# V of two head groups made in the recurrences of a fused four-layer kernel, in place of one

## The reference, cut to what matters

```python
def _cross_attention(q_in, kv_in, wq, bq, wk, bk, wv, bv, wo, bo, bias_k, bias_v):
    qh = (q_in @ wq + bq).reshape(b, q_len, H, K)
    kh = (kv_in @ wk + bk).reshape(b, t, H, K)
    vh = (kv_in @ wv + bv).reshape(b, t, H, K)
    kh = jnp.concatenate([kh, jnp.broadcast_to(bias_k, (b, 1, H, K))], axis=1)
    vh = jnp.concatenate([vh, jnp.broadcast_to(bias_v, (b, 1, H, K))], axis=1)
    logits = jnp.einsum('bqhk,bthk->bhqt', qh, kh) / scale
    weights = jax.nn.softmax(logits, axis=-1)
    ctx = jnp.einsum('bhqt,bthk->bqhk', weights, vh).reshape(b, q_len, H * K)
    return ctx @ wo + bo

x = _L0_xattn_ref(x, ctx_2048, ...)
x = _L1_xattn_ref(x, ctx_2048, ctx_2048, ...)
x = _L2_xattn_ref(ctx_2048, x, mask_BxS2_ik0, ...)
x = _L3_xattn_ref(x, ctx_2048, ...)
```

## Time and profile before

| | |
|---|---|
| median of 3 runs | 3144.73 us (3142.94 to 3148.15) |
| span of the profiled execution | 3143.0 us |
| PE busy (matmuls) | 2966.0 us, 94% |
| PE weight loads busy | 2488.1 us, 79% |
| DVE, ACT, POOL busy | 1326.3, 1117.2, 1030.7 us |
| moved | 289.75 MB, mean 92 GB/s |

### The profile page before, as it was taken

One profiled execution on the slowest core, in us unless ns is written; L12 is line 12 of the kernel. 1 busy time (PEld: TensorE's weight loads), 2 busy tenths in 40 slices (PEclk: granted clock), 3 DMA queues, 4 the chain that ended last, 5 costly groups with the idle time before them and its releaser, 6 DMA issues.

```text
span 3143.0 us, 43370 instructions
## 1 busy us (share of the span) xinstructions
PE 2966.0 (94%) x16412; PEld 2488.1 (79%) x16412; DVE 1326.3 (42%) x3062; ACT 1117.2 (36%) x2541; POOL 1030.7 (33%) x956
## 2 busy tenths in 40 slices
PE   6799888899999999999999999999989999998999
PEld 3445456888998998888989989989878877777887
DVE  4784886433333333433333333333421156563134
ACT  2333345433223222333232222232333355564332
POOL 4674674213113122222121121131245333345420
PEclk8897899999999999999999999999999999999999
DMA  6664651532122122222122222121111111111133
GB/s 214 188 195 164 199 165 44 195 119 106 60 73 106 60 73 87 73 76 78 70 93 74 73 80 73 67 106 60 53 41 67 66 45 45 43 38 58 54 114 94
DMA packets 98260, 289.75 MB, mean 92 GB/s; under 512 B 8552, under 2 KB 55144, under 8 KB 89224
## 3 DMA queue, kind: packets, MB, share of 16 engines
q1 hardware_dynamic: 97576, 286.29, 26.8%
q10 hardware_dynamic: 480, 0.69, 0.1%
HBM read 262.96 MB, written 23.99 MB: 91 GB/s over the span
## 4 chain that ended last, share of the span: by engine, by line
PE 74%; DVE 7%; ACT 6%; POOL 5%; issue 4%; DMA 3%; PEldq 0%; PEld 0%; SPq 0%; ACTq 0%; POOLq 0%; DVEq 0%
PE bank L189 21%; PE bank L191 20%; PE bank L190 20%; PE bank L1908 5%; POOL W_lo L229 3%; PE bank L1893 2%; DMA W_raw<-in_weights 2%; DVE max L2118 1%; ACT W_hi L220 1%; ACT prob L1996 1%; PE bank L2537 1%; DVE prob L2747 1%; PE bank L625 1%; POOL x L1306 1%; ACT prob L2652 1%
## 5 line engine op out<-in xcount | busy, mean ns | idle before, releaser
L2202 POOL TENSOR_SCALAR prob<-prob,inverse 112x376 f32<-112x376 f32 x256 | 144.3, 584 | 1275.1 <-DVE inverse L2124 1275.1
L229 POOL TENSOR_TENSOR W_lo<-W_raw,W_hi 128x1024 fp32r<-128x1024 f32 x138 | 329.1, 2408 | 159.7 <-ACT W_hi L220 156.1
L189 PE MATMUL bank<-ctx_hi,W_hi 128*128 128x376 f32 x1024 | 354.0, 346 | 6.8 <-DVE K_lo L271 4.2
L271 DVE SCALAR_TENSOR_TENSOR K_lo<-bank,vectors,K_hi 128x375 fp32r<-128x375 f32 (+1 forms) x288 | 172.8, 606 | 408.7 <-ACT K_hi L262 408.7
L190 PE MATMUL bank<-ctx_lo,W_hi 128*128 128x376 f32 x1024 | 343.7, 336 | 0.0
L191 PE MATMUL bank<-ctx_hi,W_lo 128*128 128x376 f32 x1024 | 343.2, 335 | 0.0
L189 PE MATMUL bank<-act_hi,W_hi 128*128 128x448 f32 x784 | 300.1, 383 | 10.5 <-DVE act_lo L269 3.6
L2069 DVE TENSOR_TENSOR V<-bank,bv 128x512 f32<-128x512 f32 x168 | 116.3, 692 | 433.6 <-PE bank L1908 235.4
L1996 ACT ACTIVATE prob<-bank,minus 112x376 f32<-112x376 f32 x256 | 143.7, 574 | 434.3 <-DVE minus L2121 434.3
L190 PE MATMUL bank<-act_lo,W_hi 128*128 128x448 f32 x784 | 293.2, 374 | 0.0
L191 PE MATMUL bank<-act_hi,W_lo 128*128 128x448 f32 x784 | 292.7, 373 | 0.0
(11 more groups left out here) (278 smaller groups left out, 6124.1 us busy)
## 6 DMA issues: line engine op xcount, KB each, us to landing
W_raw<-in_weights SPq DMA_DIRECT2D x69, 1024.0 KB, 4.9
ctx_hi<-ctx_split SPq DMA_DIRECT2D x64, 752.0 KB, 4.3
ctx_lo<-ctx_split SPq DMA_DIRECT2D x64, 752.0 KB, 5.8
v_spread<-v_rows SPq DMA_DIRECT2D x88, 224.0 KB
att<-in_ctxT SPq DMA_DIRECT2D x16, 376.0 KB, 5.3
ctx_split<-W_hi SPq DMA_DIRECT2D x16, 376.0 KB, 3.9
ctx_split<-W_lo SPq DMA_DIRECT2D x16, 376.0 KB, 4.9
W_hi<-ctx_split SPq DMA_DIRECT2D x32, 188.0 KB, 4.3
```

Source lines behind the costliest of these rows:

```text
L189: nc.tensor.matmul(dst, left[0], right[0], start=first, stop=False)
L229: pool.tensor_tensor(k.Wl[:, slot, cs, :], k.Wraw[:, cs, :], k.Wh[:, slot, cs, :].bitcast(F32), ALU.subtract).then_inc(*k.w_low.now((n, i)))
L271: dve.scalar_tensor_tensor(out=low, in0=src, scalar=bias, in1=high.bitcast(F32), op0=ALU.add, op1=ALU.subtract).then_inc(*k.banks.draining ...
L2202: pool.tensor_scalar(k.Pm[:, h, :], k.Pm[:, h, :], k.rsum[:, h:h + 1], 1.0, ALU.mult, ALU.mult).then_inc(*k.prob_done.now((n, h)))
```

## The change

`MADE` becomes 2. The fills go batch by batch, both groups of a batch after each other, on the same chunks; two quarter-tiles stand in each filling step, tile by tile. The context slot is cut into five chunks in rotation, so that the first chunk of the next batch is loaded while the present batch's four are read, and each of the others once the last tile of the second group has read the chunk whose place it takes. The second V weight gets a slot of its own (a fifth), is loaded before the first half's steps and split at steps 3 and 5 of it (`VALUES_AT`); the load of the first half's "g" weight moves from before the steps to step 5. Chunk loads are issued in the step of the matmul that frees them and stores one step earlier than they were. The attention units of group 1 become made units. A scratch area for dynamic transfers is made smaller.

```diff
-MADE = 1
-ORDER = (["v", "k", "r", "v1_0", "g", "o", "v", "r", "k"] + [f"v1_{g}" for g in range(1, MADE)] + ["g", "o", "fr", "fk"]
+MADE = 2
+ORDER = (["v", "k", "r"] + [f"v1_{g}" for g in range(MADE)] + ["g", "o", "v", "r", "k", "g", "o", "fr", "fk"]
-NSLOT = 4
+NSLOT = 5
-SLOT = ([0, 1, 0, 2, 1, 0, 1, 1, 0] + [2] * (MADE - 1) + [0, 1, 0, 2]
-        + [3, 1, 0, 2] + [(n + 3) % NSLOT for n in range(len(ORDER) - ORDER.index("q1_1"))])
+SLOT = ([0, 1, 0] + [2, 4] + [1, 0, 1, 1, 0] + [0, 1, 0, 2]
+        + [3, 1, 0, 2] + [3, 0, 2] * (MADE - 1) + [(n + 3) % 4 for n in range(len(ORDER) - ORDER.index(f"q1_{MADE}"))])
...
-FILLS = [(g, b) for g in range(MADE) for b in range(B)]
-QUANTA = [(0, c) for c in range(C)] + [(j, c) for c in range(C) for j in (1, 2)]
+FILLS = [(g, b) for b in range(B) for g in range(MADE)]
+QUANTA = [(j, c) for j in range(3) for c in range(C)]
...
+CHUNKS = 5
+
+def chunk_slot(b, c):
+    return (C * (b % HB) + c) % CHUNKS
...
-        if j == 0:
-            pe.wait_ge(k.chunk_loaded[c], 32 * (f + 1))
+        if j == 0 and g == 0:
+            pe.wait_ge(k.chunk_loaded[chunk_slot(b, c)], 32 * chunk_loads(b, c))
...
-        elif j == 2:
-            m.then_inc(*k.chunk_read.now((f, c)))
+        elif j == 2 and g == MADE - 1:
+            m.then_inc(*k.chunk_read.now((b, c)))
...
-    for q in range(made_until((half, n), 2), made_until((half, n), 1)):
+    for q in range(made_until((half, n), 1), made_until((half, n))):
         f, q = divmod(q, NQ)
-        j, c = QUANTA[q]
-        if j == 2 and (f + 1) % PER_HALF:
-            sp_chunk(k, f + 1, c)
-    for t in range(tiles_of(made_until((half, n), 3)), tiles_of(made_until((half, n), 2))):
+        (j, c), (g, b) = QUANTA[q], FILLS[f]
+        if q == 0 and g == 0 and (b + 1) % HB:
+            sp_chunk(k, b + 1, 0)
+        if j == 2 and g == MADE - 1 and (b + 1) % HB and c < C - 1:
+            sp_chunk(k, b + 1, c + 1)
+    for t in range(tiles_of(made_until((half, n), 2)), tiles_of(made_until((half, n), 1))):
...
+VALUES_AT = (3, 5)
...
+            if half == 0 and n in VALUES_AT:
+                act_split_weight(k, W_VALUES[1], (VALUES_AT.index(n),))
...
+            if half == 0 and n in VALUES_AT:
+                pool_split_weight(k, W_VALUES[1], (VALUES_AT.index(n),))
...
+            sp_load_weight(k, W_VALUES[1])
...
-        sp_load_weight(k, w["g"])
+        if half:
+            sp_load_weight(k, w["g"])
...
+            if half == 0 and n == VALUES_AT[1]:
+                sp_load_weight(k, w["g"])
...
-    nc = _bacc.Bacc("TRN2", target_bir_lowering=False, num_devices=1)
+    nc = _bacc.Bacc("TRN2", target_bir_lowering=False, num_devices=1, dynamic_dma_scratch_size=512)
```

More of the change, by code:

```diff
@@ L217, in act_split_weight, with pool_split_weight @@
         act.wait_ge(*k.banks.filled(("vf", len(FILLS) - 1, 2)))
-    for i in range(2):
+    for i in parts:
         cs = slice(2 * i, 2 * i + 2)
         act.copy(k.Wh[:, slot, cs, :], k.Wraw[:, cs, :]).then_inc(*k.w_high.now((n, i)))
-def pool_split_weight(k, n):
+def pool_split_weight(k, n, parts=range(2)):
     if n >= len(ORDER):
@@ L374, in plan_values, with chunk_loads, context_chunk @@
     for f in fills:
[L375 to L379, removed]
+        k.w_last[W_VALUES[FILLS[f][0]]] = ("vf", f, 2)
+    k.chunk_read.expect([(FILLS[f][1], c) for f in fills if FILLS[f][0] == MADE - 1 for c in range(C - 1)])
+CHUNKS = 5
+def chunk_slot(b, c):
+    return (C * (b % HB) + c) % CHUNKS
+def chunk_loads(b, c):
+    s = chunk_slot(b, c)
+    return sum(chunk_slot(*at) == s for at in CHUNK_ORDER[0:CHUNK_ORDER.index((b, c)) + 1])
+CHUNK_ORDER = [(b, c) for b in range(B) for c in range(C)]
+def context_chunk(k, b, c):
+    cols = slice(SP * chunk_slot(b, c), SP * (chunk_slot(b, c) + 1))
+    return [w[:, CONTEXT_SLOT].rearrange("p c d -> p (c d)")[:, cols] for w in (k.Wh, k.Wl)]
 TILES = [(f, j) for f in range(len(FILLS)) for j in range(3)]
 def tiles_of(quanta):
-    f, q = divmod(quanta, NQ)
-    return 3 * f + (q >= 4) + (q >= 11)
+    return quanta // C
 def pe_fill(k, half, n):
@@ L442, in sp_first_chunk, with chunk_before, sp_chunk @@
             k.nc.sync.wait_ge(k.cx_stored[s], 32 * 4 * (half + 1))
[L443 to L449, removed]
-    sp.dma_start(ch.bitcast(F32), k.cx_dram[b, 0, :, c]).then_inc(k.chunk_loaded[c], 16)
-    sp.dma_start(cl.bitcast(F32), k.cx_dram[b, 1, :, c]).then_inc(k.chunk_loaded[c], 16)
+    sp_chunk(k, HB * half, c)
+def chunk_before(b, c):
+    i = C * (b % HB) + c - CHUNKS
+    return (b // HB * HB + i // C, i % C) if i >= 0 else None
+def sp_chunk(k, b, c):
+    sp, before = k.nc.sync, chunk_before(b, c)
+    if before:
+        b0, c0 = before
+        sp.wait_ge(*(k.chunk_read[before] if c0 < C - 1 else k.banks.filled(("vf", MADE * b0 + MADE - 1, 2))))
+    ch, cl = context_chunk(k, b, c)
+    sp.dma_start(ch.bitcast(F32), k.cx_dram[b, 0, :, c]).then_inc(k.chunk_loaded[chunk_slot(b, c)], 16)
+    sp.dma_start(cl.bitcast(F32), k.cx_dram[b, 1, :, c]).then_inc(k.chunk_loaded[chunk_slot(b, c)], 16)
 def sp_value_store(k, n):
```

12 lines of the change are left out of this document (6 added, 6 removed).

## The result

| | before | after |
|---|---|---|
| median of the runs | 3144.73 us | 3152.36 us (3149.44 to 3156.77, 5 runs) |
| span of the profiled execution | 3143.0 us | 3150.1 us |
| ratio to before on the same chip, 95% interval | | 1.0035 [1.0024, 1.0045] |

The kernel became slower by 0.35%, some 11 us by the ratio. The medians in the table differ by 7.6 us and the two spans by 7.1, where the ratios give 10 to 11; a sum over one pair of traces is good to some 4 us. The forecast was 3146 in a range of 3114 to 3176. The net came out near it, but two of its terms did not, and they erred against each other. That is what the runs had to take apart.

A forecast was written before the change was run, and what follows sets the result against it. It took TensorE alone to bound attention's group 1, and TensorE, VectorE and GpSimd, chained by single-step waits, the recurrences. Terms -52 + 42 + 6 + 5 = +1 us on a 3143.0 span gave 3146 us, range 3114 to 3176.

The forecast's parts named there:

- Attention, -52: Attention stage: group 1's units no longer make V; 40.6 us from six units, 9 and 2.5 from crossings, 52 off.
- The crossing into group 2: Attention stage: this crossing becomes the kind that stood at the crossing into group 1, 34.2 us for 36.7, gaining 2.5.
- the crossing into group 1: Attention stage: this 60.0 us crossing loses 4 tiles of V, 11.0 us; with gaps, a gain of 9 us.
- Early term, 6: First half's steps 1 to 12: second V weight's split and the later load of "g" add 6 us, between 0 and 13.
- The added matmuls, 42: Recurrences, steps 13 to 60: 33.3 us of matmuls per half less 12.5 of some 17 idle used; 42 us on.
- The argument against: Recurrences, against the faster rival: VectorE picks up a block's sums one step after TensorE, so a lag stalls it at once.
- sum for a full clock: Recurrences: with the clock full throughout, TensorE's busy time would shrink by up to 7 + 11 = 18 us.
- The faster rival: Recurrences: TensorE's idle time used almost whole, wait for chunks hidden; halves grow by 25 us, total 3121; chance 0.22.
- The chunks, 5: Recurrences: shorter distance between a chunk's readers costs 0.8 us at each of six batch changes; 5 on, between 0 and 20.
- the slower rival: Recurrences: chunk loads stall TensorE and spreads, 24 us at six changes plus 8 of half clock; 3173; chance 0.22.
- the 0.8 us a turn: Recurrences, each change of batch: low half landing 7.3 us after issue against a distance of some 6.5 us; 0.8 us wait.
- Evictions and stores, 0: Recurrences: 12 more evictions per half on ScalarE and 12 more stored tiles, both hidden, costing nothing unless bursts delay spreads.

The follow-up runs named there:

- one_weight: Changed kernel with both groups using the first V weight, the second's load and split left out and "g" loaded where it was before: 1.0003, 3144.41 us.
- late_weight: Changed kernel with the second V weight loaded at step 10 and split at steps 15 and 16, after "g"; output weight later: 1.0015, 3146.28 us.
- no_reload_third: Changed kernel with no chunk replaced within a half and one matmul in place of three in the second group's quarter-tiles: 0.9871, 3101.77 us.
- no_reload_after: Changed kernel with all fills of a half reading the first batch's chunks, other batches' chunk loads left out: 0.9939, 3125.17 us.
- interleaved: Changed kernel with the second group's tiles 1 and 2 going through the chunks in pairs, freeing two chunks earlier: 1.0004, 3140.84 us.
- stores_later: Changed kernel with SP's stores of finished V tiles issued one step later, as before the change: 1.0000, 3140.22 us.
- all three edits: Changed kernel with the edits of interleaved, stores_later and late_weight together: 0.9977, 3132.18 us; also without chunk loads within a half: 0.9957, 3127.53 us.
- no_reload_before: Kernel before the change, with all fills of a half reading the first batch's chunks, other chunk loads left out: 0.9994, 3141.05 us.

## Why the prediction came out right in its net, and where its steps were wrong

**Attention, -52: right.** It measured -48.3. The six units gave 40.7, to 0.1 us what the comparison of group 0 with group 1 had said, so costing the change by the group that had already been changed was sound, and the matmuls' own 8.3 us a unit would have been too much. The crossing into group 2 gave 2.8 for 2.5. Only the crossing into group 1 was mis-sized, 4.9 for 9: with V gone from it, the weight load and the split that stood beside TensorE's work stand in the chain (7.59 us of load at 809.10), and TensorE is idle 7.7 us in place of 3.7.

**Early term, 6: right.** 6.8, and ScalarE's wait 3.14 for 3.4. one_weight shows that it is the second weight's; in late_weight's trace it goes where the split goes.

**The added matmuls, 42: too large.** Without chunk loads the growth over before is 13.6 + 10.5 = 24 us, and no_reload_third shows that nearly all of it is the 192 matmuls that it leaves out. The term was the added busy time, 66 us, less the idle time used, "12.5 of some 17 us" a half. The idle time was the smaller mistake: TensorE idled 36.5 us in the two stretches before and 7.6 in no_reload_after (121.5 busy of 123.5 us, 117.3 of 122.9), so 29 us were used and not 25. The argument against, that VectorE needs the sums one step later, did not hold at this size. The busy time was the larger one: it grew by 53 us (238.8 less 185.8) and not 66. With the mean granted clock up from 0.92 and 0.88 to 0.95 and 0.97, the prediction's own sum for a full clock (18 us to be had) gives an estimate of 9 of these 13 us; the other 4 are not traced. The prediction held the clock for an argument of the faster rival alone and left it out of its term. That rival, priced at 25 us of growth, had this part right to 1 us, but no sum is given for its 25 (all idle time used gives 31, a full clock 18 less), so the closeness is partly luck. The rule of the Trainium skill that it cited ("Perfetto Trace Analysis", Identifying the Most-Contended Engine), by which weight loads tell the headroom, would have given no growth at all. The trace does not agree: 24 us of growth with weight loads busy 74.5 of 123.5 us. The idle time of the matmul row was the better guide here.

**The chunks, 5: too small, and out of the bounds given (0 to 20).** They cost 27 us, near what the slower rival had said (24 for six turns and 8 of half clock). Its sign was that waits for chunks or spreads exceed 25 us. TensorE's own waits for chunks show 16.2 us and VectorE's for spreads 17 (11.2 in the row above and 6.0 for `tmp`), so neither did. The rest of the 27 us is mostly the clock: in the stretches of after TensorE is idle 22.3 us and busy 251.3, without chunk loads 7.6 and 238.8. So 15 us of the cost are idle time and 12 are the same matmuls taking longer, at 0.94 and 0.92 in place of 0.95 and 0.97 (by the mean clocks, as above, an estimate of 8 of the 12); the matmul at 202.40 is one of those at the half clock. The rival's mechanism was half right. It had the landing as what decides, at about 7 us. The landings measured in after's first half are shorter than before, not longer:

```profile
DMA to landing us min/median/max: 2.5/4.5/7.5
```

4.5 us in the median against 7.3 in the earlier trace rows (5.4 against 7.2 in the second half). The step that failed is the 0.8 us a turn: a landing of 7.3 us less a distance of "2.5 steps, some 6.5 us". At the turn shown above the landing took 5.83 us, and from the last reader's end to the moment at which TensorE wants the chunk there were 5.3 us; these two alone would give 0.5. But the load was issued 2.1 us after its place was free, and the wait was 2.65. The estimate left out the time that SP takes to get to the load, behind two other pairs, a store and a spread; SP's rows in the section on the change show them standing there. interleaved (9 us), which sets the third pair alone, and stores_later (11 us, of which the store's 0.5 us a turn explains a part) shorten that time, and with all three edits 5.3 us of chunk cost are left, the size that the step had given. What the term left out beside it is the lower clock behind each wait.

**Evictions and stores, 0**: as work, right to 2 us by no_reload_third. As a place in SP's queue, stores were not free while chunk loads stood behind them (stores_later).

**Net.** 42 + 5 predicted, 24 + 27 measured: 47 and 51. The forecast's time stood because two terms erred by some 20 us each, against each other, and that is luck. The faster rival is what is left when the chunks' cost is taken away: it gave 24 us less than before, and no_reload_after measured 19 less (0.0061 of 3143).

**Open.** The stretch between the recurrences and the attention stage became 3.6 us shorter with no edit to it; TensorE is busy 2.7 us less in it and its mean clock is 0.94 where it was 0.91. What raised the clock there was not tested. Nor was it tested why the three edits without loads are slower than the plain order without loads in the second half, nor what in stores_later gave more than the store's own issue at the turns.

## What to carry to other kernels

When a buffer's refill gets a shorter reuse distance, count the distance from the moment at which the issuing queue gets to it, behind every issue and every wait that stands ahead of it there, and not from the moment at which the buffer is free; here the landings became shorter and the wait for them still grew. Work added to an engine that idles in lumps and may run ahead used four fifths of the idle time; and its own price fell with the idle time, since the busy time grew by 53 us where the matmuls at the full clock stand for 66. In reverse, a wait that is added costs more than its length: 15 us of idle time came with 12 us of slower matmuls. A net that agrees with the forecast proves no term: take out one suspect at a time, then both, since here either alone hid part of the other.

## What the runs showed of the hardware that was not expected

- More work on TensorE did not lower its granted clock; the mean was lower where TensorE idled more: 0.92 and 0.88 in the stretches before (36.5 us idle), 0.95 and 0.97 with 96 more quarter-tiles and no waits for chunks (7.6 us), 0.88 and 0.88 with a third of the added matmuls and waits for chunks (37.3 us). Idle time alone does not order them all: the second half of no_reload_before stood at 0.85 with 14.9 us idle, below the 0.88 of before with 19.4. The Trainium skill ("TensorE: Matmul & The Clock Gate", Part 1) says that activity releases the throttle, and these rows agree as far as they go.
- The time from issue to landing of the same 188 KB load ran from 2.5 to 7.5 us within one stretch, median 4.5, at a DMA share of 0.57; before, at 0.63, 2.8 to 8.3, median 7.3.
- A transfer takes its turn on SP even when it waits for nothing: each issue stood 0.3 to 0.6 us there, and the third pair of chunk loads went out 3.4 us after the first issue of the first pair, 2.9 with one store less between them. SP's long waits for ScalarE's evictions, 134 us in after and 159 in no_reload_after, did not stand in front of these loads.
